# Expert output bias laid out beside the weights and added on VectorE, with a ring of eight weight loads

## The reference

```
h = silu(x @ W1[e] + b1[e]) * (x @ W11[e] + b11[e])
y = y + (h @ W2[e] + b2[e]) * gates[:, e]
z = silu(x @ Ws1 + bs1) * (x @ Ws11 + bs11) @ Ws2 + bs2      # shared
out = x + y + z
```

## Time and profile before

| | us |
|---|---|
| median of 3 runs | 332.52 |
| the profiled execution: its time | 332.63 |
| its span, first to last instruction | 330.8 |
| TensorE busy | 273.5 |
| VectorE busy | 216.1 |
| ScalarE busy | 161.7 |
| GpSimd busy | 126.5 |
| expert loop, first product to last | 241.1 to 314.5 |

### The profile page before, as it was taken

One profiled execution on the slowest core, in us unless ns is written; L12 is line 12 of the kernel. 1 busy time (PEld: TensorE's weight loads), 2 busy tenths in 40 slices (PEclk: granted clock), 3 DMA queues, 4 the chain that ended last, 5 costly groups with the idle time before them and its releaser, 6 DMA issues.

```text
span 330.8 us, 6002 instructions
## 1 busy us (share of the span) xinstructions
PE 273.5 (83%) x1821; PEld 203.9 (62%) x1837; DVE 216.1 (65%) x718; ACT 161.7 (49%) x317; POOL 126.5 (38%) x203
## 2 busy tenths in 40 slices
PE   0138799899989899898998879988899999999900
PEld 0025455465646466464664456877789999999900
DVE  7976846675575787757887568792455565555606
ACT  1412556555596465864648646541244444444300
POOL 0324134333412333555337200737025665666620
PEclk9999999999999999999999999999999999999965
DMA  7999500000000000000001000106417759484137
GB/s 270 374 398 400 205 2 0 1 2 2 2 0 2 0 0 4 24 24 18 0 3 40 24 2 1 51 26 178 136 40 214 229 159 263 138 249 130 65 117 287
DMA packets 21711, 33.75 MB, mean 102 GB/s; under 512 B 2656, under 2 KB 11584, under 8 KB 21552
## 3 DMA queue, kind: packets, MB, share of 16 engines
q1 hardware_dynamic: 19152, 28.15, 26.6%
q0 software_dynamic: 2528, 5.22, 4.6%
HBM read 23.90 MB, written 9.45 MB: 101 GB/s over the span
## 4 chain that ended last, share of the span: by engine, by line
PE 64%; DVE 18%; ACT 7%; issue 5%; DMA 4%; SPq 1%; POOL 1%; POOLq 0%; ACTq 0%; DVEq 0%
PE ps L1392 7%; PE ps L1374 6%; PE ps L1380 6%; DVE mpad L582 6%; PE ps L1304 5%; PE ps L1116 4%; PE ps L1144 4%; PE ps L1158 4%; PE ps L1117 4%; PE ps L1076 3%; PE ps L1078 3%; PE ps L1077 3%; PE ps L1154 3%; PE ps L1129 3%; PE ps L1142 3%
## 5 line engine op out<-in xcount | busy, mean ns | idle before, releaser
L582 DVE TENSOR_REDUCE mpad<-ps 128x2 f32<-128x308 f32 x128 | 55.2, 472 | 31.7 <-PE ps L1117 31.0
L824 POOL TENSOR_SCALAR ks<-k_stack,cst 128x160 fp32r<-128x160 f32 x64 | 29.8, 479 | 93.8 <-DVE k_stack L567 93.8
L897 POOL DMA_INDIRECT result_rows<-yo,dest x47 | 45.4, 966 | 41.1 <-DVE yo L798 40.8
L962 ACT ACTIVATE pf<-ps 128x512 f32<-128x512 f32 x80 | 46.4, 597 | 13.2 <-PE ps L1158 9.9
L1117 PE MATMUL ps<-ks,qs 96*128 96x308 f32 x128 | 46.1, 416 | 0.0
L863 POOL DMA_INDIRECT slot_rows<-xr,slot x32 | 31.4, 983 | 35.5 <-DVE slot L485 27.0
L1116 PE MATMUL ps<-mq_b,identb 128*128 128x308 bf16 x128 | 38.8, 308 | 4.5 <-DVE mpad L582 3.5
L1144 PE MATMUL ps<-qs,ks 128*128 128x512 f32 x64 | 37.2, 583 | 1.2 <-ACT pf L962 1.2
L1116 PEld LDWEIGHTS ps<-mq_b,identb 128*128 128x128 bf16 x128 | 12.5, 98 | 32.7 <-issue 26.0
L789 DVE SCALAR_TENSOR_TENSOR e_h<-ps,wu,e_s 128x128 f32<-128x128 f32 x62 | 18.9, 346 | 19.9 <-PE ps L1380 18.9
L1063 ACT ACTIVATE e_s<-ps,wu 128x128 f32<-128x128 f32 x62 | 19.4, 363 | 25.2 <-PE ps L1374 25.2
(11 more groups left out here) (200 smaller groups left out, 614.9 us busy)
## 6 DMA issues: line engine op xcount, KB each, us to landing
wu<-w_up SPq DMA_DIRECT2D x31, 258.0 KB, 3.6
wr<-w_up SPq DMA_DIRECT2D x1, 4128.0 KB, 21.2
slot_rows<-zero SPq DMA_DIRECT2D x1, 3120.0 KB, 24.3
xg<-slot_rows SPq DMA_DIRECT2D x12, 260.0 KB, 4.3
wd<-w_down SPq DMA_DIRECT2D x1, 2048.0 KB, 11.0
xo<-result_rows SPq DMA_DIRECT2D x4, 512.0 KB, 5.4
xs<-x SPq DMA_DIRECT2D x1, 1024.0 KB, 4.8
out<-xs SPq DMA_DIRECT2D x4, 256.0 KB, 2.3
```

What stands on the lines that cost most here:

```text
L582: dve.tensor_reduce(mpad[:, m % 2, q, 96 + 2 * a:98 + 2 * a], ps[:, KS_ + a, 0:2 * SK].rearrange("p (c k) -> p c k", c=2), AX.X, ALU.max, ...
L824: pool.tensor_scalar(ks[:, HG * (m % 4) + j, :], k_stack[:, m % 2, :], cst[:, C_SELM + j:C_SELM + j + 1], cst[:, C_SELO + j:C_SELO + j + 1 ...
L897: pool.indirect_dma_start(out=result_dram[:, :], out_offset=bass.IndirectOffsetOnAxis(ap=dest[:, n:n + 1], axis=0), in_=yo[:, n % 4, :], i ...
L962: act.activation(pf[:, n % RP, :], ps[:, ST_ + n % 2, :], ACT.Exp, scale=DK ** -0.5).then_inc(exp_done, 1)
```

## The change

The bias no longer goes through TensorE. The host lays `b2[e]`, repeated on all 128 partitions, behind the up weights of each expert, so a row of `w_up` grows from 516 to 644 floats (WU). DVE adds `bs2` (now on 128 partitions) to these columns of the resident copy in four steps, one at the end of each group of batch 0. The result is written back to a DRAM tensor `w_dram`, from which the ring is loaded. In the loop `result` becomes two DVE instructions, an addition that reads PSUM and the weights' bias columns, and the scaling. The weights of a tile are thus in use until its result is done, so the ring's wait is on `yo_done`, and the ring has eight buffers.

```diff
-WU = 2 * H + 4
+WB = 2 * H + 4
+WU = WB + D
-RW = 6
+RW = 8
...
+        w_dram = nc.dram_tensor("w_biased", (NE, P, WU), F32, kind="Internal").ap()
...
-            sp.dma_start(b_raw[:, :], b_rows).then_inc(ld_b, 16)
             sp.dma_start(bsr[:, :], bs_rows).then_inc(ld_b, 16)
...
                 if d >= RW:
-                    sp.wait_ge(eh_done, 2 * (ring[d - RW] + 1))
-                sp.dma_start(wu[:, d % RW, :], w_up[bass.ds(e, 1), :, :].rearrange("a p n -> (a p) n")
+                    sp.wait_ge(yo_done, ring[d - RW] + 1)
+                sp.dma_start(wu[:, d % RW, :], w_dram[bass.ds(e, 1), :, :].rearrange("a p n -> (a p) n")
                              ).then_inc(ld_u[d % RW], 16)
 
+            sp.wait_ge(biased, NG)
+            sp.dma_start(w_dram.rearrange("e p n -> p e n"), wr[:, :, :]).then_inc(w_kept, 16)
+            sp.wait_ge(w_kept, 16)
             sp.wait_ge(tile_known, 1)
...
-            def bias_step(k):
...
+            def add_biases(i):
+
+                rows = wr[:, 4 * i:4 * i + 4, WB:WB + D]
+                dve.tensor_tensor(rows, rows, bsr[:, :].unsqueeze(1).to_broadcast([P, 4, D]), ALU.add).then_inc(biased, 1)
...
-                    if b == 0 and g in (1, 2):
-                        if g == 1:
-                            dve.wait_ge(ld_b, 32)
-                            link(dve.tensor_tensor(b_raw[:, :], b_raw[:, :], bsr[:, :], ALU.add))
-                        for k in range(5 * g - 5, 5 * g):
-                            bias_step(k)
+                    if b == 0:
+                        if g == 0:
+                            dve.wait_ge(ld_b, 16)
+                            dve.wait_ge(ld_d, 32)
+                        add_biases(g)
...
-                dve.tensor_scalar(tile_one[:, :], ps[:, M_, 0:TILES], cst[:, C_WHO:C_WHO + 1], None, ALU.is_equal)
...
-                dve.tensor_scalar(yo[:, n % 4, :], ps[:, Y_ + n % 2, 0:D], gate[:, n:n + 1], None,
+                dve.tensor_tensor(y_b[:, n % 2, :], ps[:, Y_ + n % 2, 0:D], up_weights(n)[:, WB:WB + D],
+                                  ALU.add).then_inc(y_summed, 1)
+                dve.wait_ge(y_summed, n + 1)
+                dve.tensor_scalar(yo[:, n % 4, :], y_b[:, n % 2, :], gate[:, n:n + 1], None,
                                   ALU.mult).then_inc(yo_done, 1)
...
-                pe.matmul(o, tile_one[:, block_of(n):block_of(n) + 1].to_broadcast([P, P]), b_all[:, :], start=True, stop=False)
                 for c in range(2):
                     last = pe.matmul(o, e_h[:, n % RH, P * c:P * c + P],
                                      wd[:, bass.ds(e, 1), D * c:D * c + D].rearrange("p a n -> p (a n)"),
-                                     start=False, stop=c == 1)
+                                     start=c == 0, stop=c == 1)
...
-            pe.wait_ge(b_step, 10)
```

More of the change, by code:

```diff
@@ L45 @@
 XW = D + 2
-NB = 3 * NE
 C_ID = 0
@@ L61 @@
 C_QUAD = C_DEST + 2 * NT
-C_PART = C_QUAD + HG
-C_WHO = C_PART + 3
-C_ROW = C_WHO + 1
+C_ROW = C_QUAD + HG
 C_FIRST = C_ROW + 1
@@ L124, in build @@
 def build(nc, x, ctx_t, wq, wk, wv, wo, mask_q, mask_k, bias_cols, bv_rows, bo_rows, bs_rows, wg,
-          b_rows, w_shared, w_up, w_down, consts, out):
+          w_shared, w_up, w_down, consts, out):
     stack = ExitStack()
@@ L157, in build @@
         zero = sb("zero", [P, FILL * XW])
-        bsr = sb("bsr", [NB, D])
+        bsr = sb("bsr", [P, D])
         wg_s, wg_hl = sb("wg_s", [P, NE]), sb("wg_hl", [P, 2 * NE], F32R)
@@ L164, in build @@
         wr = sb("wr", [P, NE, WU])
-        b_raw = sb("b_raw", [NB, D])
-        b_part, b_sel = (sb(n, [NB, D], BF16) for n in ("b_part", "b_sel"))
-        b_all = sb("b_all", [P, D], BF16)
+        y_b = sb("y_b", [P, 2, D])
         attention = ExitStack()
@@ L210, in build @@
         te = sb("te", [1, TILES], I32)
-        tile_one = sb("tile_one", [P, TILES], BF16)
         xg = sb("xg", [P, 2, 4, XW])
@@ L236, in build @@
          q_part_done, qs_done, smax_mm, max_done, mt_mm, qmax_done, st_mm, exp_done, pv_mm, os_done, ot_mm,
-         on_done, ont_mm, ont_done, x1_mm, x1_done, w_split, b_step, lg_done, ex_in, ex_done, copied, sel_done,
+         on_done, ont_mm, ont_done, x1_mm, x1_done, w_split, lg_done, ex_in, ex_done, copied, sel_done,
          rank_mm, rank_read, slots_done, sent, tile_known, te_summed, te_mm, a_mm, b_mm, silu_done, h_done, w2_mm,
          x2_done, tx_mm, xgt_done, meta_done, gate_mm, lin_mm, esilu_done, eh_done,
-         ey_mm, yo_done, out_done, stored, ld_d) = (sem(n) for n in (
+         ey_mm, yo_done, out_done, stored, biased, w_kept, y_summed, ld_d) = (sem(n) for n in (
             "ld_x ld_c ld_w ld_m ld_ctx ld_b zeroed dve_step cleared scanned "
@@ L245, in build @@
             "max_done mt_mm qmax_done st_mm exp_done pv_mm os_done ot_mm on_done ont_mm ont_done x1_mm x1_done "
-            "w_split b_step lg_done ex_in ex_done copied sel_done rank_mm rank_read slots_done sent tile_known te_summed te_mm a_mm b_mm "
+            "w_split lg_done ex_in ex_done copied sel_done rank_mm rank_read slots_done sent tile_known te_summed te_mm a_mm b_mm "
             "silu_done h_done w2_mm x2_done tx_mm xgt_done meta_done "
-            "gate_mm lin_mm esilu_done eh_done ey_mm yo_done out_done stored ld_d").split())
+            "gate_mm lin_mm esilu_done eh_done ey_mm yo_done out_done stored biased w_kept y_summed ld_d").split())
         ld_f = [sem(f"ld_f{par}") for par in range(2)]
@@ L513, in _ @@
                 dve.memset(v[:, 0, :], float(first))
-            dve.memset(b_all[:, :], 0.0)
             link(dve.memset(zero[:, :], 0.0))
@@ L1439, in constants @@
         c[:, C_DEST + NT * k:C_DEST + NT * k + NT] = SLOTS + 2 * (NT * p[:, None] + np.arange(NT)) + k
-    for r in range(3):
-        c[:, C_PART + r] = p // NE == r
     c[:, C_ROW] = p
-    c[:, C_WHO] = np.where(p < NB, p % NE, -1)
     return c
@@ L1478 @@
     biases = np.concatenate([np.asarray(v).reshape(NE, 2, P) for v in (L0_ffn_b1, L0_ffn_b11)], axis=1).transpose(0, 2, 1)
+    b2 = np.tile(np.asarray(L0_ffn_b2).reshape(NE, 1, D), (1, P, 1))
     arrays = {
@@ L1490 @@
         "bo_rows": np.tile(np.asarray(L0_xattn_bo), (P, 1)),
-        "bs_rows": np.tile(np.asarray(L0_ffn_bs2), (NB, 1)),
+        "bs_rows": np.tile(np.asarray(L0_ffn_bs2), (P, 1)),
         "wg": L0_ffn_Wg,
-        "b_rows": np.tile(np.asarray(L0_ffn_b2), (3, 1)),
         "w_shared": np.concatenate([w1, w11, chunks(L0_ffn_Ws2)], axis=2),
-        "w_up": np.concatenate([L0_ffn_W1, L0_ffn_W11, biases], axis=2),
+        "w_up": np.concatenate([L0_ffn_W1, L0_ffn_W11, biases, b2], axis=2),
         "w_down": chunks(L0_ffn_W2),
```

## The result

| | before | changed |
|---|---|---|
| median, us | 332.82 (4 runs, 330.97 to 333.23) | 355.38 (4 runs, 352.31 to 358.77) |
| profiled execution: time, span | 332.63, 330.8 | 354.77, 353.0 |

The ratio is 1.064, with a 95% interval of 1.059 to 1.069: slower by some 22 us. The run of 358.77 us, more than 1.5% above the fastest of its kernel, counts in the median and not in the ratio.

The account below looks back on a forecast made before the run. The prediction took TensorE, busy 83% of the span, as the bound: 332.6 - 5.2 (product) - 0.8 (batch 0) + 0.4 (end) + 17.9 (waits) + 4 (clock) = 348.9, 349 us, slower; range 337 to 366, the forecast's own 338 to 355.

Parts of the forecast that it names:

- the rival with the falling clock: Expert loop: same waits for rows, but TensorE's clock falls at most of them; 356 to 367 us, chance 34%.
- The product: Expert loop, TensorE: the bias product and its weight load go, 0.11 us for each of 47 tiles, 5.2 us gained.
- The addition on DVE: Result step of each tile: the added DVE instruction costs nothing in the loop, 0.4 us at the end.
- Batch 0: Head groups of batch 0: bias steps go, four additions come; net -0.8 us, ends -2.0 and +0.8.
- The wait that moves: SP's queue: rows behind the later ring wait have a lead of 1.10 us, so TensorE waits 17.9 us in all.
- The clock: Expert loop: TensorE's clock falls at two of the new waits, at 2 us each, +4 us.
- the forecast's own sign: Expert loop: a granted clock under 1.00 decides between the forecast and the rival with the falling clock.
- the 22 us that the forecast put beside the rule: Expert loop: cost if the clock falls at all eight waits, as the skill's rule would have it, instead of 4.
- faster: Transposes of the rows: TensorE never waits for xg, so the 17.9 and 4 us go; 327.0 us, chance 10%.
- DVE becomes the bound: Expert loop: TensorE waits for DVE's hidden or result while rows are in time; 332 us, chance 6%.

Follow-up runs that it names:

- e1: Changed kernel with the rows of a group issued at n = 4g - 2, ahead of that place's ring load, not at 4g + 1: 328.55 us, ratio 0.985.
- e2: Changed kernel with the rows of a group issued one place earlier, at n = 4g instead of 4g + 1: 338.42 us, ratio 1.015.
- e3: Kernel before with one line changed: the ring load waits for yo_done, not eh_done: 348.65 us, ratio 1.047.
- e4: Kernel before without the bias product of the experts (b2 and bs2 missing in the output): 328.01 us, ratio 0.985.
- e7: Kernel before without the eleven DVE bias instructions of batch 0 (b2 and bs2 missing in the output): 331.44 us, ratio 0.995.
- e6: Changed kernel with the rows issued early as in e1 and a ring of six instead of eight: 330.67 us, ratio 0.991.
- e8: Changed kernel with filling TensorE products ahead of all eight waits for rows (8, 10 or 5 each): 350.17 us, ratio 1.056.
- e5: Changed kernel with eight filling TensorE products ahead of the waits of groups 3, 4, 6, 7, 9 and 10: 350.14 us, ratio 1.048.
- e9: The changed kernel run again unaltered, beside e8 on the same chip: 355.81 us, ratio 1.070.

## Why the prediction was right, point by point

The forecast was 349 us by the waits with a clock that mostly holds, and the rival with the falling clock 356 to 367. The changed kernel came at 355.38, between the two and just under the rival. The step on which the forecast rests, the rows behind SP's later wait, was right, and e1, e2 and e3 show it. The sizes are less good, and the terms measured as follows.

- **The product**: -5.2 forecast, -5.1 in e4.
- **The addition on DVE**: nothing in the loop forecast, and e1 shows it. Its two instructions are shorter than I took them, 0.28 and 0.29 us for 0.35 and 0.34. At the end +0.4 was forecast. Behind group 11 the changed kernel takes 26.63 us and e4, without the product and without the addition, 26.46: about +0.2, from one execution of each.
- **Batch 0**: -0.8 forecast. The head groups show -1.3, and e7 1.8 for the steps alone, so the four additions show 0.5 to 0.7 together, where 1.2 was taken. The larger load of the up weights landed after 24.1 us (26.5 at most forecast), and the write-back, sent at 78.46, after 16.8 (26.5); neither shows in the path, as forecast.
- **The opening**: no term in the forecast. The loop starts 0.9 later and not 0.8 earlier, because the maximum at 50.37 is 2.36 us late. Of these, 0.4 are there when the products of 25.4 start, and 1.3 before the clock falls at 39: TensorE came to its full speed later. From 30 to 35 us it has 20 records in the changed kernel and 25 in e2, which has the same opening:

```profile
30.00:35.00 5.00, 5.00 (x20) 3.72 (x18) 3.37 (x8) 1.26 (x2) 2.27 (x5) 1.00 1.04 409
```

```profile
30.00:35.00 5.00, 5.00 (x25) 3.65 (x23) 3.43 (x9) 1.26 (x2) 2.25 (x5) 1.00 1.04 409
```

The column of the granted clock reads 1.00 in both, and also where the forecast read half the clock from the earlier trace rows; it does not show this first rise, which only the durations show (L1065 on 128x128: 0.41 us at 34.54, 0.28 at 69.25). The fall at 39 then costs the last 1.1 us. It isn't a fixed cost: in the profiled e2, e6 and e8, with the same opening, the slow products end by 33.8 us, the clock does not fall, and the first transposes come at 238.3 to 238.7, before the 239.73 of the kernel before. In the changed kernel, e1, e5 and e9 the slow products last until 34.7 to 35.7 us, and the clock falls. In the four profiled executions with the old opening neither happens. Why the speed comes later in some executions was not tried.
- **The wait that moves**: lead 1.10 us forecast, 1.25 measured at group 3; waits at groups 3 to 10, except 5, and none at 11, where all eight were forecast. Their sum was 17.9 forecast and 16.7 measured, but those are not the same thing, and the nearness is luck, since slow stretches shorten the wait behind them: group 5 waited nothing behind a fall. e8 shows the sum as it was reckoned, at full clock: 73.85 us less nine groups of 5.79 is 21.7. Groups 3, 6 and 9 take 8.40, 8.23 and 8.29 us (5.79 + 2.3 = 8.1 forecast), groups 5 and 8 take 7.06 and 6.94 (7.0 forecast), and groups 4, 7 and 10 take 9.81, 9.48 and 9.79, where 5.79 + 2.9 = 8.7 was forecast. So their landing was mis-sized: 4.0 taken, and in e8 the rows of groups 4, 7 and 10 landed after 5.1, 4.7 and 5.0 us, below the largest of the earlier trace rows, 5.5.
- **The clock**: +4 for two falls forecast; four and five falls came, at a cost of 4.2 to 6.8 us. In the changed kernel they came in or right behind the waits of 2.52, 2.30, 3.86 and 3.18 us, and not at those of 2.15 and 2.05 us; e3, with falls behind 1.90 us and none behind 2.29, shows that this is no order by length. The price of one fall, 1 to 1.4 us, is below the 2 that I took, because the slow stretch hides in the next wait; their number was above. That 4 is near 4.2 is therefore luck: twice the falls at half the price. By the forecast's own sign, a clock under 1.00 in the loop, its first rival came true at half of the waits, at a lower price than the rival's. The Trainium skill ("TensorE: Matmul & The Clock Gate", "HAM oscillation") says that a loop in which each round's products take less time than the wait for the next DMA loses the full clock in every round. Here a round has 5.79 us of products and waits of 2 to 4 us, so this loop is not the page's case, and the 22 us that the forecast put beside the rule did not come; falls came all the same, at four and five of eight waits.

Against 348.9 the profiled 354.8 is 5.9 more: 1.7 in the opening, and 4.0 in the nine groups, 78.05 where 52.1 + 17.9 + 4 = 74.0 was forecast. By e8 nearly all of the 4.0, 3.8 us, is the waits that were reckoned too short, most of it at groups 4, 7 and 10. The rivals "faster" and "DVE becomes the bound" needed a lead that is longer than any landing, or a DVE that TensorE waits for; e1 has the first and shows that the second does not follow.

## What to carry to other kernels

A queue that runs in order makes every transfer wait for the slowest condition ahead of it: when a buffer is released later, look not at the transfer that refills it but at what is queued behind, and reckon its lead against its landing time. The changed kernel had the deeper ring already and lost 6.4%; moving the independent load ahead of the wait turned that into -1.5%. The depth still has to be reckoned for itself, as e6 shows.

## What the runs showed of the hardware

A fallen clock hides partly in the next wait for a DMA, so that its price is less than the work it slows: about 17 us at half the clock in the loop of the changed kernel cost 4.2 us against e8. Its fall does not go by the length of one wait (1.90 us and 2.29 us in e3), and it stays away when TensorE has products to do there (e8). The granted clock of the profile reads 1.00 before TensorE first comes to full speed, so there only durations tell. And the scaling of 128x128 fp32 on DVE takes 0.29 us when it reads SBUF where it took 0.34 from PSUM, so the second instruction cost less than its own length.
